# Seeding PSUM banks for Strassen sums in a fused cross-attention and expert FFN kernel

## The chip, the cores and the metric

The kernel runs on one core of a Trainium2 chip. The metric is the device time of one execution in microseconds, taken as the median of several runs.

## The reference

`x` is (16, 112, 256), `ctx` is (16, 375, 256), all in fp32. After a layer norm, one cross attention with biases is added to `x`, and after a second layer norm an expert FFN with 8 experts, all of which see all 1792 tokens:

```python
x = x + xattn(layernorm(x), ctx, Wq, bq, Wk, bk, Wv, bv)
g = einsum('bsh,ehf->ebsf', x_, w_gate)      # x_ = layernorm(x)
u = einsum('bsh,ehf->ebsf', x_, w_up)        # 8 experts, 256 -> 1024
h = silu(g) * u
expert_out = einsum('ebsf,efh->ebsh', h, w_down)
out = einsum('ebsh,bse->bsh', expert_out, cw)  # cw from two softmaxes
```

## The kernel before

**Precision.** Every operand of a matmul is split into a high part (rounded to fp32r) and a low part (the rest), and a product is three matmuls: high x high, high x low, low x high (`three`, `accumulate`, L355). The high part of a tile is a ScalarE copy (`high_...`), the low part a GpSimd subtraction (`low_...`).

**Stages.** An attention stage comes first. The FFN then goes through 64 quads, numbered n. A quad makes the hidden tiles of one pair of 128-wide column blocks of one half expert, for one half of the tokens (two blocks of 448 tokens). Four quads (turn = n mod 4) are one half expert `hn`: turns 0 and 1 are token half 0, turns 2 and 3 token half 1; turns 0 and 2 use one weight set, 1 and 3 the next. Quads 0 to 3 use eight plain products per matrix; quads 4 to 63 use Strassen's seven products P1 to P7, for gate and for up (`product`, L2001). In the text "gate 6" is product P6 of gate.

**Sums.** With Winograd's form of the sums, C11 = P1 + P2, U2 = P1 + P6, U3 = U2 + P7, C22 = U3 + P5, C21 = U3 + P4, C12 = U2 + P5 + P3. Each matrix has three PSUM banks: a, x and y. P1 is made in bank a and P2 is added there by the matmuls, P6, P7 and P4 come in x one behind another, P5 and P3 in y. P1 is copied to SBUF by ScalarE (`gate_first`, `up_first`, through L1060), and VectorE makes five sums per matrix (L1466 to L1503), those of x and y against the tile kept in SBUF. P7, P4 and P3 accumulate on what their bank holds. The hidden tiles are Silu(gate) times up, four per quad (L1505 to L1523, `hidden11` reads C11 of up from PSUM; the other three read two SBUF tiles), then their high part (L1087), then their low part (L702), into one of four `hs` slots.

**Down.** A group g = n // 2 - 1 of two quads is multiplied with the down weights while the next two quads run. For groups 2 to 29 this is four units of 12 matmuls of 448 columns (`unit`, L2072): 0 and 1 in the even quad, 2 and 3 in the odd one. VectorE weighs a unit by the combine weights (L1556) and GpSimd adds it up (L819). The other groups (0, 1, 30, 31) use seven tiles of 12 matmuls of 256 columns (`down`), which VectorE adds up with the weight (L1541). For group 31 each tile is made in two halves, `earlier` (quad 62's part) and `later` (quad 63's part), after the last quad.

**Order.** There is no scheduler: each engine has its own list of calls, written by hand, in a function `quad(n)` (GpSimd L829, ScalarE L1254, VectorE L1763, TensorE L2272), and waits on semaphores stand in the helpers. An instruction that waits holds up all behind it on its engine. TensorE's order in a quad is: gate 1, 6, 5; up 1, 6, 5; unit 2 if n is odd; gate 2, 7; up 2, 7; gate 4, 3; unit 0 if n is even; up 4, 3; unit 3 or 1. ScalarE also makes the high parts of the weight sets (`high_set`, L1017, 1792 columns) and down weights (`high_down`, L1027); GpSimd makes the sums of weights (L681) and the low parts of sets (L691) and of down weights (L696). Weight set 2hn must be ready at turn 0 of half expert hn, set 2hn + 1 at turn 1 (`gate_1_6_5`, L2007). The loads come on SyncE's queue, in program order, each when its buffer is free.

Of the kernel before, what the change touches and what calls it, by code (L numbers as in the profile page):

```python
# [5 lines left out]
def xattn_ffn_kernel(nc, x, ctx, wq, bq, wk, bk, wv, bv, w_router, w_gating, w_gate, w_up, w_down, out):  # L6
# [3 lines left out]
    B, TQ, D = x.shape  # L10
# [38 lines left out]
    LAST = (4, 5, 6, 0, 1, 2, 3)  # L49
# [26 lines left out]
    PROD = {p: i + 1 for i, p in enumerate((1, 6, 5, 2, 7, 4, 3))}  # L76
    U2_SUM, U3_SUM, C22_SUM, C21_SUM, C12_SUM = range(1, 6)
    HID11, HID22, HID21, HID12 = range(1, 5)
# [17 lines left out]
    with es:  # L96
# [90 lines left out]
        u21 = [up_t[:, 0, :], sb("u21_odd", [P, TC])[:, :]]  # L187
        u12 = [up_t[:, 1, :], xsacc[:, TILES * D:TILES * D + TC]]
        g21, g12, g22, g11 = [gate_t[:, i, :] for i in range(4)]
        u22 = up_t[:, 2, :]  # L190

        blocks = [u21[1][:, 0:CB * Q], w_raw0[:, 0, 4:8, :].rearrange("p s f -> p (s f)")[:, 0:CB * Q]]
# [4 lines left out]
        plain_tile = [g11, g12, g21, g22]  # L197
# [70 lines left out]
        ps_end = [ps[:, i, 0:D] for i in (3, 4, 5, 6, 1, 2, 0)]  # L268
# [44 lines left out]
        gate_prod, up_prod, gate_p1, up_p1 = sem("gate_prod"), sem("up_prod"), sem("gate_p1"), sem("up_p1")  # L313
# [17 lines left out]
        def unit_at(g, k):  # L331

            c, block = 1 - k // 2, k % 2
            return acc_t[:, g % CP, block, c * TC:(c + 1) * TC]
# [37 lines left out]
        def _(sp):  # L372
# [222 lines left out]
            for a, b, count in ((4, RT, 3), (0, 2, 5), (2, 3, 6), (3, 4, RT)):  # L595
                sp.wait_ge(acc_done, RT * (CP + 1) + count)
                sp.dma_start(out_v[:, RT + a:RT + b, :], last_acc[1][:, a:b, :]).then_inc(stored, DMA)
            sp.wait_ge(stored, 5 * DMA)
        @block.gpsimd
        def _(pool):  # L600
# [228 lines left out]
            def quad(n):  # L829
# [17 lines left out]
                if turn == 0:  # L847
                    low_set(2 * hn + 1)
                if turn == 1 and hn + 1 < SETS:
# [5 lines left out]
                if turn == 3 and hn + 1 < SETS:  # L855
                    low_set(2 * hn + 2)
# [5 lines left out]
                low_hidden(n, HID22, u22, 1, TC)  # L862
# [3 lines left out]
            low_hidden(QUADS - 1, HID21, u21[1], 0, TC)  # L866
            low_hidden(QUADS - 1, HID12, u12[1], 1, 0)
            add_back(1)
        @block.scalar
        def _(sc):  # L870
# [183 lines left out]
            def before(n, k):  # L1054

                return 4 * n if n == PLAIN else 4 * (n - 1) + k

            def first_product(n, prod, dst, bank, done):
# [3 lines left out]
            def gate_first(n):  # L1062
                if n == PLAIN:
                    sc.wait_ge(hid_lo_done, 4 * n)
                sc.wait_ge(hid_done, before(n, HID21))
                first_product(n, gate_prod, g21, g_a, gate_p1)

            def up_first(n):
                if n > PLAIN + 1:
                    sc.wait_ge(hid_lo_done, 4 * (n - 2) + HID21)  # L1070
                first_product(n, up_prod, u21[n % 2], u_a, up_p1)

            def activate11(n):
                sc.wait_ge(gate_prod, 7 * (n - PLAIN) + PROD[2])
                sc.wait_ge(hid_lo_done, before(n, HID11))
                nc.scalar.activation(g11, g_a, ACT.Silu).then_inc(act_done, 1)  # L1076

            def activate(n, tile, sums):
                sc.wait_ge(gate_sum, 5 * (n - PLAIN) + sums)
# [174 lines left out]
            def quad(n):  # L1254
# [3 lines left out]
                gate_first(n)  # L1258
                if n > PLAIN:
                    high_hidden(n - 1, HID21, u21[(n - 1) % 2], 0, TC)  # L1260
                up_first(n)
                if n > PLAIN:
                    high_hidden(n - 1, HID12, u12[(n - 1) % 2], 1, 0)
                if n == PLAIN:
                    high_part(1, "s13")
                if n == PLAIN + 1:
                    high_part(1, "s2")
                    high_part(1, "s4")
                if turn == 0:
                    high_set(2 * hn + 1)  # L1270
# [1102 lines left out]
```

## Time and profile before

| | |
|---|---|
| median of 3 runs | 964.14 us (962.96 to 965.56) |
| span of the profiled execution | 961.7 us |
| that execution's own time | not given by the page |
| TensorE matmul busy | 956.4 us, 5089 instructions |
| VectorE busy | 744.5 us, 1280 instructions |
| ScalarE busy | 483.2 us, 855 instructions |
| GpSimd busy | 797.4 us, 640 instructions |

The span runs from the first to the last instruction on the chip; the time of a run also holds what lies around it. In a row of a timeline the columns are: start in us from the span's start, length in us, engine and line, operation, output <- inputs, count, and in brackets the idle time of the engine ahead of it with what ended it. PE is TensorE's matmuls, PEld its weight loads, which run beside matmuls, DVE VectorE, ACT ScalarE, POOL GpSimd. An engine's neighbouring instructions can overlap, so that one starts before the one ahead of it has ended.

### The profile page before, as it was taken

The numbers are of one execution on the slowest core, as the hardware profiler recorded it, in microseconds if no ns is written. First come the engines' busy times: TensorE is split into PE (matmuls) and PEld (weight loads), VectorE is DVE, ScalarE is ACT, GpSimd is POOL, SyncE is SP. The second block draws the span as 40 slices with busy tenths as digits, with TensorE's granted clock in tenths as the row PEclk, the third lists the DMA queues.
The fourth block names the chain that finished last, engine by engine and source line by source line (L and its number), as shares of the span: only waits on it lengthen the run. The fifth ranks groups of instructions, "written<-read, shape, count | busy, mean of one in ns | idle before, by whom it ended". The sixth has DMA issues, their size and how long they took to land.

```text
span 961.7 us, 14792 instructions
## 1 busy us (share of the span) xinstructions
PE 956.4 (99%) x5089; PEld 887.8 (92%) x5089; DVE 744.5 (77%) x1280; ACT 483.2 (50%) x855; POOL 797.4 (83%) x640
## 2 busy tenths in 40 slices
PE   9999999999999999999999999999999999999998
PEld 7999899999999999999999999999999999999998
DVE  4997557787877877788877787778877778777995
ACT  6987544454545444444544444445445454445442
POOL 5899976766888888888988888888898888888885
DMA  7472512311010110021100110011100200111135
GB/s 217 119 171 73 145 38 75 109 64 42 22 44 23 42 62 24 22 64 42 44 22 23 45 61 22 23 64 42 45 23 22 74 31 23 36 51 42 39 51 141
DMA packets 73232, 55.85 MB, mean 58 GB/s; under 512 B 30244, under 2 KB 69485, under 8 KB 73158
## 3 DMA queue, kind: packets, MB, share of 16 engines
q1 hardware_dynamic: 73150, 54.91, 19.6%
q8 instruction: 40, 0.66, 0.3%
q14 instruction: 34, 0.28, 0.1%
q10 hardware_dynamic: 8, 0.00, 0.0%
HBM read 46.58 MB, written 6.48 MB: 55 GB/s over the span
## 4 chain that ended last, share of the span: by engine, by line
PE 98%; DMA 1%; ACT 0%; DVE 0%; issue 0%; SPq 0%; DVEq 0%; ACTq 0%
PE ps L355 96%; PE ps L1878 1%; DMA xf<-in_L_xattn_Wk 1%; PE ps L1914 0%; PE ps L1866 0%; PE ps L1931 0%; DVE early L1350 0%; ACT arena L912 0%; PE ps L1957 0%; ACT xf L920 0%; ACT xf L912 0%; ACT early L899 0%; PE ps L1824 0%; DVE arena L366 0%; ACT arena L920 0%
## 5 line engine op out<-in xcount | busy, mean ns | idle before, releaser
L355 PE MATMUL ps<-arena 128*128 128x448 f32 (+5 forms) x2064 | 388.4, 339 | 0.2
L355 PEld LDWEIGHTS ps<-arena 128*128 128x128 f32 (+2 forms) x2064 | 343.6, 186 | 21.4 <-POOL arena L696 0.4
L702 POOL TENSOR_TENSOR arena<-shared,arena 128x448 fp32r<-128x448 f32 x196 | 252.3, 1301 | 120.6 <-ACT arena L1087 116.8
L355 PE MATMUL ps<-xc_hi,w_hi 128*128 128x448 f32 x904 | 330.6, 366 | 0.0
L355 PE MATMUL ps<-xc_hi,w_lo 128*128 128x448 f32 x904 | 330.2, 365 | 0.0
L355 PE MATMUL ps<-xc_lo,w_hi 128*128 128x448 f32 x904 | 330.2, 365 | 0.0
L355 PEld LDWEIGHTS ps<-xc_hi,w_lo 128*128 128x128 f32 x904 | 169.8, 188 | 13.6
L355 PEld LDWEIGHTS ps<-xc_hi,w_hi 128*128 128x128 f32 x904 | 169.8, 188 | 13.3
L355 PEld LDWEIGHTS ps<-xc_lo,w_hi 128*128 128x128 f32 x904 | 169.9, 188 | 13.2
L1080 ACT ACTIVATE shared<-shared 128x448 f32<-128x448 f32 x180 | 101.5, 580 | 145.5 <-DVE shared L1476 73.9
L819 POOL TENSOR_TENSOR xsacc<-xsacc,xf 128x448 f32<-128x448 f32 x104 | 119.3, 1158 | 0.0
L1087 ACT CAST arena<-shared 128x448 fp32r<-128x448 f32 x180 | 101.8, 569 | 27.4 <-DVE shared L1513 27.4
L1060 ACT COPY shared<-ps 128x448 f32<-128x448 f32 x90 | 48.0, 533 | 133.3 <-PE ps L355 106.9
L1556 DVE TENSOR_TENSOR xf<-ps,xf 128x448 f32<-128x448 f32 x104 | 61.9, 617 | 58.7 <-PE ps L355 58.7
L1470 DVE TENSOR_TENSOR shared<-ps,shared 128x448 f32<-128x448 f32 x60 | 37.5, 625 | 48.7 <-PE ps L355 48.7
L1076 ACT ACTIVATE shared<-ps 128x448 f32<-128x448 f32 x60 | 32.8, 546 | 78.9 <-PE ps L355 78.9
L691 POOL TENSOR_TENSOR w_lo<-w_raw,w_hi 128x1792 fp32r<-128x1792 f32 (+1 forms) x17 | 66.1, 3886 | 0.4 <-ACT w_hi L1017 0.4
L1513 DVE TENSOR_TENSOR shared<-shared 128x448 f32<-128x448 f32 x60 | 65.9, 1098 | 0.0
L691 POOL TENSOR_TENSOR w_lo<-early,w_hi 128x1792 fp32r<-128x1792 f32 x15 | 61.2, 4078 | 2.4 <-ACT w_hi L1017 2.4
L1466 DVE TENSOR_TENSOR shared<-ps,shared 128x448 f32<-128x448 f32 x60 | 37.0, 617 | 30.2 <-ACT shared L1060 29.8
L681 POOL TENSOR_TENSOR w_raw<-w_raw 128x256 f32<-128x256 f32 x60 | 46.8, 802 | 1.2
L681 POOL TENSOR_TENSOR early<-early 128x256 f32<-128x256 f32 x60 | 43.7, 750 | 2.4 <-DMA early<-in_L_ffn_w_up 1.2
(168 smaller groups left out, 1154.3 us busy)
## 6 DMA issues: line engine op xcount, KB each, us to landing
early<-in_L_ffn_w_down SPq DMA_DIRECT2D x16, 512.0 KB, 3.8
xf<-cw_dram SPq DMA_DIRECT2D x16, 448.0 KB, 4.7
shared<-in_ctx SPq DMA_DIRECT2D x16, 336.0 KB
w_raw<-in_L_ffn_w_gate SPq DMA_DIRECT2D x17, 256.0 KB, 2.8
w_raw<-in_L_ffn_w_up SPq DMA_DIRECT2D x17, 256.0 KB, 3.2
early<-in_L_ffn_w_gate SPq DMA_DIRECT2D x15, 256.0 KB, 2.9
early<-in_L_ffn_w_up SPq DMA_DIRECT2D x15, 256.0 KB, 3.1
xsacc<-in_x SPq DMA_DIRECT2D x8, 224.0 KB, 6.2
```

Of the source, the lines that this page charges most:

```text
L355: ins = nc.tensor.matmul(dst, w, m, start=first and i == 0, stop=last and i == len(passes) - 1, skip_group_check=onto)
L681: nc.gpsimd.tensor_tensor(s[dst], s[a], s[b], ALU.subtract).then_inc(t_step[n % 2], 1)
L691: nc.gpsimd.tensor_tensor(w_lo[:, n % FPAIRS, :, used, :], raw[:, :, src, :], w_hi[:, n % FPAIRS, :, used, :].bitcast(fp32), ALU.subtract) ...
L702: nc.gpsimd.tensor_tensor(h[:, 1, j, at:at + TC], tile, h[:, 0, j, at:at + TC].bitcast(fp32), ALU.subtract).then_inc(hid_lo_done, 1)
L819: nc.gpsimd.tensor_tensor(to, to, weighed[u % 2], ALU.add).then_inc(unit_done, 1)
L1060: nc.scalar.copy(dst, bank).then_inc(done, 1)
L1080: nc.scalar.activation(tile, tile, ACT.Silu).then_inc(act_done, 1)
L1087: nc.scalar.copy(hs[n % HSLOTS][:, 0, j, at:at + TC], tile).then_inc(hid_hi_done, 1)
L1466: nc.vector.tensor_tensor(g12, g_x, g21, ALU.add).then_inc(gate_sum, 1)
L1470: nc.vector.tensor_tensor(g22, g_x, g21, ALU.add).then_inc(gate_sum, 1)
L1513: nc.vector.tensor_tensor(u22, g22, u22, ALU.mult).then_inc(hid_done, 1)
L1556: nc.vector.tensor_tensor(to, ps_unit[u % 2], cw_all[:, g % CP, c * TC:(c + 1) * TC], ALU.mult).then_inc(weighed_done, 1)
```

## The change

P1 is no longer added by VectorE. ScalarE writes P1 from bank a into bank x (`gate_seed`, `up_seed`), and P6, P7 and P4 all accumulate on it, so x holds U2, then U3, then C21. ScalarE copies P5 out of y (`keep5`) and U2 out of x (`keep2`) into SBUF; P3 accumulates on P5 in y. VectorE makes two sums per matrix: C22 = x + kept P5, C12 = y + kept U2 (up's C12 is written into bank y). Gate's C21 goes to Silu from PSUM, up's C21 and C12 are read by the hidden products from PSUM. Up's x bank gets one extra matmul ahead of its first use (`prime`). The order of the hidden tiles is 11, 22, 12, 21, and units 0 and 1 now make the first token block. Semaphores `gate_kept` and `up_kept` count the three ScalarE copies (SEEDED, KEPT5, KEPT2). The hidden tiles that alternate between two buffers are gate's, not up's.

The core of the diff:

```diff
-    LAST = (4, 5, 6, 0, 1, 2, 3)
+    LAST = (0, 1, 2, 4, 5, 6, 3)
-    PROD = {p: i + 1 for i, p in enumerate((1, 6, 5, 2, 7, 4, 3))}
+    PROD = {p: i + 1 for i, p in enumerate((1, 5, 6, 2, 7, 3, 4))}
...
-            for a, b, count in ((4, RT, 3), (0, 2, 5), (2, 3, 6), (3, 4, RT)):
+            for a, b, count in ((0, 3, 3), (4, 6, 5), (6, RT, 6), (3, 4, RT)):
...
 # GpSimd, quad(n)
                 if n > PLAIN:
-                    low_hidden(n - 1, HID21, u21[(n - 1) % 2], 0, TC)
-                    low_hidden(n - 1, HID12, u12[(n - 1) % 2], 1, 0)
+                    low_hidden(n - 1, HID21, g21, 0, TC)
...
                 low_hidden(n, HID11, g11, 0, 0)
-                low_hidden(n, HID22, u22, 1, TC)
+                low_hidden(n, HID22, g22[n % 2], 1, TC)
+                low_hidden(n, HID12, g12[n % 2], 1, 0)
...
 # ScalarE
+            def seed(n, prod, bank, onto, done):
                 sc.wait_ge(prod, 7 * (n - PLAIN) + PROD[1])
-                nc.scalar.copy(dst, bank).then_inc(done, 1)
+                nc.scalar.copy(onto, bank).then_inc(done, 1)
+            def gate_seed(n):
+                seed(n, gate_prod, g_a, g_x, gate_kept)
+            def up_seed(n):
+                sc.wait_ge(hid_done, 4 * n)
+                seed(n, up_prod, u_a, u_x, up_kept)
+            def gate_keep5(n):
+                sc.wait_ge(gate_prod, 7 * (n - PLAIN) + PROD[5])
+                if n >= PLAIN + 2:
+                    sc.wait_ge(hid_lo_done, 4 * (n - 2) + HID22)
+                nc.scalar.copy(g22[n % 2], g_y).then_inc(gate_kept, 1)
+            def gate_keep2(n):
+                sc.wait_ge(gate_prod, 7 * (n - PLAIN) + PROD[6])
...
+                nc.scalar.copy(g12[n % 2], g_x).then_inc(gate_kept, 1)
...
 # ScalarE, quad(n)
                 if turn == 2 and hn > 1:
                     high_down(hn)
-                gate_first(n)
-                if n > PLAIN:
-                    high_hidden(n - 1, HID21, u21[(n - 1) % 2], 0, TC)
-                up_first(n)
-                if n > PLAIN:
-                    high_hidden(n - 1, HID12, u12[(n - 1) % 2], 1, 0)
+                gate_seed(n)
+                gate_keep5(n)
+                up_seed(n)
+                up_keep5(n)
                 if n == PLAIN:
                     high_part(1, "s13")
+                    high_set(2 * hn + 1)
+                gate_keep2(n)
+                activate11(n)
+                up_keep2(n)
                 if n == PLAIN + 1:
                     high_part(1, "s2")
                     high_part(1, "s4")
-                if turn == 0:
-                    high_set(2 * hn + 1)
-                if turn == 3 and hn + 1 < SETS:
-                    high_set(2 * hn + 2)
+                high_hidden(n, HID11, g11, 0, 0)
                 if turn == 2 and hn == 1:
                     high_down(hn)
-                activate11(n)
-                activate(n, g22, C22_SUM)
-                activate(n, g21, C21_SUM)
-                activate(n, g12, C12_SUM)
-                high_hidden(n, HID11, g11, 0, 0)
-                high_hidden(n, HID22, u22, 1, TC)
+                activate(n, g22[n % 2], C22_SUM)
+                activate(n, g12[n % 2], C12_SUM)
+                high_hidden(n, HID22, g22[n % 2], 1, TC)
+                high_hidden(n, HID12, g12[n % 2], 1, 0)
+                activate21(n)
+                high_hidden(n, HID21, g21, 0, TC)
+                if turn == 2 and hn + 1 < SETS:
+                    high_set(2 * hn + 2)
+                if turn == 3 and hn + 1 < SETS:
+                    high_set(2 * hn + 3)
...
 # VectorE, quad(n)
-                gate_u2(n)
...
                 if odd and g in TURNED:
-                    weigh(g, 0)
                     weigh(g, 1)
+                    weigh(g, 2)
...
-                up_u2(n)
...
-                gate_u3_c22(n)
+                hidden11(n)
+                gate_c22(n)
+                gate_c12(n)
                 if odd and g not in TURNED:
                     add_rows(g, 2, ps_r[2])
                     add_rows(g, 3, ps_r[3])
+                up_c22(n)
+                hidden22(n)
+                up_c12(n)
+                hidden12(n)
                 if n == QUADS - 2:
-                    turn(1, 1)
                     turn(1, 2)
-                up_u3_c22(n)
-                gate_c21_c12(n)
-                hidden11(n)
-                hidden22(n)
...
                     turn(1, 3)
-                up_c21(n)
-                up_c12(n)
+                if not odd and g in TURNED:
+                    weigh(g, 0)
                 hidden21(n)
-                hidden12(n)
...
 # TensorE
-            def gate_2_7(n):
-                pe.wait_ge(gate_p1, n - PLAIN + 1)
+            def gate_6_2(n):
+                pe.wait_ge(gate_kept, 3 * (n - PLAIN) + SEEDED)
+                product(n, 0, 6, g_x, False).then_inc(gate_prod, 1)
                 product(n, 0, 2, g_a, False).then_inc(gate_prod, 1)
+            def gate_7_3(n):
+                pe.wait_ge(gate_kept, 3 * (n - PLAIN) + KEPT2)
                 product(n, 0, 7, g_x, False).then_inc(gate_prod, 1)
+                product(n, 0, 3, g_y, False).then_inc(gate_prod, 1)
+            def gate_4(n):
+                pe.wait_ge(gate_sum, 2 * (n - PLAIN) + C22_SUM)
                 product(n, 0, 4, g_x, False).then_inc(gate_prod, 1)
...
+            def up_4(n):
+                pe.wait_ge(up_sum, 2 * (n - PLAIN) + C22_SUM)
                 product(n, 1, 4, u_x, False).then_inc(up_prod, 1)
...
 # TensorE, quad(n)
-                gate_1_6_5(n)
+                gate_1_5(n)
...
-                up_1_6_5(n)
+                up_1_5(n)
...
                 if odd and turned:
                     unit(g, 2)
-                gate_2_7(n)
+                gate_6_2(n)
                 if odd and by_tile:
                     down(g, 3)
-                up_2_7(n)
-                gate_4_3(n)
+                up_6_2(n)
+                gate_7_3(n)
+                up_7_3(n)
                 if odd and by_tile and n < QUADS - 1:
                     down(g, 4)
                 if not odd and turned:
                     unit(g, 0)
                 if n == QUADS - 2:
                     down(g, 0)
-                up_4_3(n)
+                gate_4(n)
+                up_4(n)
```

After the last quad, TensorE's halves of group 31 come in the order earlier 0, 1, 2, 4; later 0, 1, 2; earlier 5, 6; later 4, 5, 6; earlier 3, later 3, with a wait for the tile that each needs.

## Rows read from the trace of the kernel before

**Rows 1.** The page: busy time, share of the span, instructions.
```profile
PE 956.4 (99%) x5089; PEld 887.8 (92%) x5089; DVE 744.5 (77%) x1280; ACT 483.2 (50%) x855; POOL 797.4 (83%) x640
```

**Rows 2.** Stretches: length, busy us (instructions) of each engine, PEclk, DMA share, GB/s.
```profile
400.00:500.00 100.00, 100.00 (x495) 92.66 (x495) 78.11 (x120) 47.78 (x81) 85.25 (x64) 1.00 0.12 38
...
945.00:961.70 16.70, 14.01 (x117) 13.79 (x115) 8.47 (x16) 2.36 (x5) 10.13 (x11) 1.00 0.39 120
```

**Rows 3.** Waits of TensorE's matmuls, the longest: us in total, times, longest.
```profile
PE ps L1976 <- DVE logits_room L1600: 1.1, 1, 1.1
```

**Rows 4.** Timeline, TensorE: quads 34, 35 and 36 start at 547.15, 560.53, 573.90.
```profile
547.15 0.37 PE L355 MATMUL ps<-xc_hi,w_hi 128*128 128x448 f32 x1
...
567.41 0.19 PEld L355 LDWEIGHTS ps<-xc_hi,w_lo 128*128 128x128 f32 x1
567.62 0.36 PE L355 MATMUL ps<-xc_hi,w_lo 128*128 128x448 f32 x1
...
573.90 0.36 PE L355 MATMUL ps<-xc_hi,w_hi 128*128 128x448 f32 x1
```

**Rows 5.** Timelines of DVE, ACT and POOL over quads 33 to 35.
```profile
541.27 0.63 DVE L1470 TENSOR_TENSOR shared<-ps,shared 128x448 f32<-128x448 f32 x1 [0.59 <-PE ps L355]
541.93 0.62 DVE L1472 TENSOR_TENSOR shared<-ps,shared 128x448 f32<-128x448 f32 x1
...
545.28 0.62 DVE L1513 TENSOR_TENSOR shared<-shared 128x448 f32<-128x448 f32 x1
...
550.44 0.62 DVE L1488 TENSOR_TENSOR shared<-ps,shared 128x448 f32<-128x448 f32 x1 [0.20 <-ACT shared L1060]
...
556.22 1.16 DVE L1513 TENSOR_TENSOR shared<-shared 128x448 f32<-128x448 f32 x1
...
568.02 0.62 DVE L1470 TENSOR_TENSOR shared<-ps,shared 128x448 f32<-128x448 f32 x1 [0.59 <-PE ps L355]
...
542.58 0.58 ACT L1080 ACTIVATE shared<-shared 128x448 f32<-128x448 f32 x1 [1.38 <-DVE shared L1472]
...
549.84 0.53 ACT L1060 COPY shared<-ps 128x448 f32<-128x448 f32 x1 [0.49 <-PE ps L355]
...
563.64 0.57 ACT L1087 CAST arena<-shared 128x448 fp32r<-128x448 f32 x1
564.11 1.70 ACT L1017 CAST w_hi<-early 128x1792 fp32r<-128x1792 f32 x1
...
546.04 2.66 POOL L702 TENSOR_TENSOR arena<-shared,arena 128x448 fp32r<-128x448 f32 x2 [1.09 <-ACT arena L1087]
...
554.75 3.23 POOL L681 TENSOR_TENSOR w_raw<-w_raw 128x256 f32<-128x256 f32 x4
```

**Rows 6.** Three lines by themselves: count, duration in ns (least/median/most), first and last.
```profile
L1513 DVE TENSOR_TENSOR shared<-shared x60: 618/1155/1986, 154.2 to 945.0; 128x448 f32<-128x448 f32 x60
...
L696 POOL TENSOR_TENSOR arena<-early,arena x16: 2407/2791/2802, 121.0 to 923.2; 128x1024 fp32r<-128x1024 f32 x16
...
L702 POOL TENSOR_TENSOR arena<-shared,arena x196: 1142/1159/1639, 99.3 to 946.9; 128x448 fp32r<-128x448 f32 x196
```

**Rows 7.** Timelines of quads 4 (ACT) and 6 (PE, ACT, POOL, PEld).
```profile
146.74 0.94 ACT L994 CAST xc_hi<-xf 128x896 fp32r<-128x896 f32 x1
...
171.27 1.60 PE L355 MATMUL ps<-arena 128*128 128x256 f32 x12
...
176.22 1.05 ACT L1027 CAST arena<-early 128x1024 fp32r<-128x1024 f32 x1 [1.65 <-PE ps L355]
177.35 2.41 POOL L696 TENSOR_TENSOR arena<-early,arena 128x1024 fp32r<-128x1024 f32 x1 [1.54 <-ACT arena L1027]
...
179.81 1.11 PEld L355 LDWEIGHTS ps<-arena 128*128 128x128 f32 x6 [0.41 <-POOL arena L696]
```

**Rows 8.** Timeline of the end: DVE's row additions, and TensorE after the last quad.
```profile
941.00 0.88 DVE L1541 SCALAR_TENSOR_TENSOR early<-ps,cw,early 128x256 f32<-128x256 f32 x2 [0.15 <-PE ps L355]
...
944.45 14.56 PE L355 MATMUL ps<-arena 128*128 128x256 f32 x120
```

More of the change, by code:

```diff
@@ L1063, in gate_first @@
                 if n == PLAIN:
                     sc.wait_ge(hid_lo_done, 4 * n)
[L1065 to L1071, printed above, removed]
+                else:
+                    sc.wait_ge(up_sum, 2 * (n - PLAIN))
+                nc.scalar.copy(u2, u_x).then_inc(up_kept, 1)
@@ L1073, in activate11, with activate21 @@
             def activate11(n):
                 sc.wait_ge(gate_prod, 7 * (n - PLAIN) + PROD[2])
-                sc.wait_ge(hid_lo_done, before(n, HID11))
+                sc.wait_ge(hid_lo_done, 4 * n if n == PLAIN else 4 * (n - 1) + HID11)
                 nc.scalar.activation(g11, g_a, ACT.Silu).then_inc(act_done, 1)
+            def activate21(n):
+                sc.wait_ge(gate_prod, 7 * (n - PLAIN) + PROD[4])
+                sc.wait_ge(hid_lo_done, 4 * n)
+                nc.scalar.activation(g21, g_x, ACT.Silu).then_inc(act_done, 1)
@@ L1785, in quad @@
                     turn(1, 0)
-                if odd and g in TURNED:
-                    weigh(g, 2)
+                    turn(1, 1)
                 if not odd and g - 1 not in TURNED:
                     add_rows(g - 1, 6, ps_r[6])
-                gate_u3_c22(n)
+                hidden11(n)
+                gate_c22(n)
+                gate_c12(n)
                 if odd and g not in TURNED:
@@ L2005, in product, with prime, gate_1_5 @@
                                   first=first, onto=not first)
-            def gate_1_6_5(n):
+            def prime(bank):
+                nc.tensor.matmul(bank, w_hi[:, 0, 0, 0, :], xc_hi[:, 0, 0, :], start=True, stop=True)
+            def gate_1_5(n):
                 hn, turn = n // (CP * FPAIRS), n % (CP * FPAIRS)
@@ L2328, in _ @@
             pe.wait_ge(hid_lo_done, last)
-            pe.wait_ge(gate_sum, 5 * (QUADS - PLAIN))
-            earlier(4)
+            pe.wait_ge(act_done, last + HID11)
+            earlier(0)
+            pe.wait_ge(gate_sum, 2 * (QUADS - PLAIN))
+            earlier(1)
+            pe.wait_ge(hid_done, last + HID11)
+            earlier(2)
+            pe.wait_ge(hid_done, last + HID12)
+            earlier(4)
+            pe.wait_ge(hid_lo_done, last + HID12)
+            later(0)
+            later(1)
+            later(2)
+            pe.wait_ge(act_done, last + HID21)
             earlier(5)
-            pe.wait_ge(act_done, last + HID11)
+            pe.wait_ge(hid_done, last + HID21)
             earlier(6)
-            pe.wait_ge(hid_done, last + HID11)
-            earlier(0)
             pe.wait_ge(hid_lo_done, last + HID21)
@@ L2340, in _ @@
             later(6)
-            pe.wait_ge(up_sum, 5 * (QUADS - PLAIN))
-            earlier(1)
-            earlier(2)
-            pe.wait_ge(hid_lo_done, last + HID12)
-            later(0)
-            later(1)
             pe.wait_ge(acc_done, RT * CP + 6)
             earlier(3)
-            later(2)
             later(3)
```

142 lines of the change are left out of this document (61 added, 81 removed).

## The prediction, made before the changed kernel was run

> **What bounds the kernel now.** I read the page's busy shares first: TensorE is busy 99% of the span [rows 1]. The table of stretches says how full: the granted clock is 1.00, there are about 495 matmuls in each 100 us of the Strassen stage, and idle time only in the last 16.7 us [rows 2]. The list of waits of TensorE has three entries, the longest of 1.1 us, all of them on lines of the attention stage [rows 3]. One wait more, not in that list, shows as a weight load 0.41 us late at 179.81, behind POOL's low part of the down weights [rows 7]. From matmul to matmul it takes 26.75 us / 132 = 0.2027 us over two whole quads [rows 4]. A quad is 14 products of 3 matmuls and two units of 12, so 66 x 0.2027 = 13.38 us, and a product is 0.61. TensorE therefore issues all the time. DVE, ACT and POOL have idle time (77%, 50%, 83% busy), and work taken off them buys nothing unless TensorE waits for it. The change can win almost nothing and can lose wherever an operand of a product comes late. So the question is only: which of the new waits is not met?
>
> **How I put times on the new order.** A few steps, read from rows, carry it. From the start of a product's last matmul to the start of the DVE or ACT instruction that reads it: 567.62 to 568.02, 0.40 [rows 4, 5]. From the start of a DVE sum to one that needs its result: 541.27 to 541.93, 0.66; to an ACT instruction that needs it: 541.93 to 542.58, 0.65 [rows 5]. Independent DVE neighbours follow at 0.53 (two sums of 0.62 overlap) [rows 5]. ACT copy to a dependent DVE sum: 549.84 to 550.44, 0.60 [rows 5]; I take 0.62 behind a Silu. ACT after ACT: the next starts 0.10 before the end, 0.47 behind a high part of 0.57 (563.64 to 564.11), so 0.43 behind a copy of 0.53 [rows 5]. ACT to POOL: 0.08 behind the end (176.22 + 1.05 to 177.35), so 0.65 for a high part [rows 7]. An event on POOL releases the weight load 0.05 later (177.35 + 2.41 = 179.76 to 179.81) [rows 7]; in steady running the weight load starts 0.20 ahead of its matmul [rows 4].
>
> **The part that costs: from an odd quad into the next even one.** The first product that accumulates on a seeded bank, gate 6, must wait for ScalarE's seed. In an even quad nothing stands between up 5 and gate 6, so its first matmul is due 12 x 0.2027 = 2.43 us into the quad, its weight load at 2.23. Counted from the start of the odd quad before it: 78 x 0.2027 - 0.20 = 15.61. In an odd quad unit 2 (12 matmuls) stands ahead of gate 6, so the sums come late, 4.86 us and more after its start. Follow the last of them. Up 7 is products 44 counted in matmuls: its last starts at 8.92, so up's C22 sum starts at 9.32. Hidden 22 follows at 9.98, up's C12 sum at 10.51, hidden 12 at 11.17, high part 12 on ACT at 11.82, Silu 21 behind it at 12.29 (gate 4 was ready at 10.5), hidden 21 on DVE at 12.91, high part 21 at 13.56, and the next ACT instruction at 14.03. In turn 3 (the turn is the quad's number mod 4) that is now the high part of a weight set, which the change moved here from behind up's copy, where it was harmless. It lasts 1.70 [rows 5]: 14.03 + 1.60 = 15.63. Only then comes the gate seed: 0.53, and 0.05 to the weight load: 16.21. Due was 15.61. **TensorE waits 0.60 us.** There are 14 such places (quads 8, 12 ... 60): 14 x 0.60 = 8.4 us. In turn 2 the high part of the down weights stands ahead of the seed instead, 1.05 long [rows 7]: 14.03 + 0.95 + 0.53 + 0.05 = 15.56, met by 0.05. I cost these 14 at nothing; the cover is thin, and each 0.1 us more in the chain makes 1.4 us at them and 1.4 at the others. From an even quad into an odd one unit 2 covers everything: gate 6 is due 2.43 later and the sums come 2.43 earlier.
>
> What is queued behind the late seed on ACT are keep 5, up's seed, keep 5 of up, gate's keep 2. They follow at 0.43 each, and gate 7, due 12 matmuls (2.43 us) after gate 6, still gets its keep in time, since gate 6 itself moved by the same wait.
>
> Two prices in the chain are not shown by a row. The seed writes PSUM, which no ScalarE row of before does: nearest are the copy out of PSUM (0.53) and the same size from SBUF to SBUF (0.57) [rows 5]. I take 0.53, the row with the same source, and bound it by 0.43 and 0.75, since another source moved it by only 0.04; that is -1.4 us (14 places) to +5.5 (28 places, as the turn-2 ones then count too). The Trainium skill (ScalarE: Activation LUTs, Step-by-step) says an ACTIVATE into PSUM is quicker than one into SBUF; by that the seed's price would sit at or below 0.53. It gives no size, and no row here shows it. The second is hidden 22, whose two inputs both lie in SBUF: rows of its kind run from 0.62 to 1.99, median 1.16 [rows 6]. A 0.62 one stands where POOL is between instructions (545.28, POOL idle until 546.04), the 1.16 one beside POOL's weight sums [rows 5]. In the new order POOL's low part 11 starts at 8.79 (up 2's last matmul 7.09, + 0.40, + 0.65, + 0.65) and ends 1.14 to 1.16 later [rows 6] at 9.95 or before, just ahead of 9.98, and low part 22 can't start before hidden 22 is done. So I take 0.62. The Trainium skill (SBUF — State Buffer, two separate sides) calls that shared port an exclusive lock in which the later of the two blocks until the first is done. By that rule an overlap of 0.1 us would cost 0.1, and only a POOL still busy with its weight set would cost 0.5 or more. The rows' 1.16 beside POOL agree with a delay, and a run of four short ones, 3.23 us long, let it in before its end.
>
> **Once only.** (a) Quad 6, down weights of the second half. ACT's high part of them moves from before Silu 11 to behind high part 11. Quad 6 starts at 171.27 - 9 x 0.2027 = 169.45, with two down tiles of 1.45 each in it (12 x 0.12) [rows 7, 8]. Gate 6 now starts 4 products and 2 tiles in, at 5.33; up 2's last matmul at 7.56, hidden 11 at 7.96, high part at 8.61, the down weights' high part at 9.08, POOL's low part at 10.21, its end at 12.62 (2.41; others of its kind take 2.79 [rows 6]), load at 12.67. Due: 5.33 + 24 x 0.2027 - 0.20 = 9.99. Wait 2.7, of which before already has 0.41: **+2.3** (2.7 with the long form). (b) Quad 63: two row additions (0.88 [rows 8]) now stand between gate's C12 sum and up's C22 sum, which up 4 needs at once, with no down tile or unit between. Gate 3's last matmul lies 10 matmuls ahead of up 4, so C12 starts at -1.63, the additions at -1.10, up's C22 at -0.23, its end and load at +0.44, due -0.20: **+0.65**. Quad 5 has the same additions, but a down tile of 1.45 covers them. (c) The priming matmul: **+0.2**. (d) Quad 4: a part and a weight set (0.94 and 1.70 [rows 5, 7]) now stand on ACT ahead of gate's keep 2. Up's keep 5 starts 4.08 in, then 4.51, 5.35, keep 2 at 6.95, end 7.48, load due 7.58: met. (e) The tail: 120 narrow matmuls without a gap [rows 8]. In the new order the last high part 21 is ready about 3.5 us and its low part 4.8 us after up 4, needed after three down tiles and seven half-tiles, over 9 us. The last store is again a single tile behind the last addition, so what follows TensorE's last matmul doesn't change.
>
> **Costed at nothing.** Six sums of 0.62 fewer and four copies of 0.53 more per quad take DVE's busy time down by at least 6 x 60 x 0.62 = 223 us and ACT's up by 4 x 60 x 0.53 = 127 us, to about 610 (63%). POOL's 16 low parts per four quads stay. Its weight sets, sums and units keep their turns, and the high parts that it waits for come earlier, so the loads on SP's queue, which wait for POOL, are not later. The turn of the last rows in quads 61 and 62 falls into DVE's idle time; the copies back have the rest of quad 62 and all of 63.
>
> **Sum.** 8.4 + 2.3 + 0.65 + 0.2 = 11.6 us, on a span of 961.7. The page does not give that execution's own time; the median of the runs is 964.1, 2.4 us above the span, and their spread is 2.6 us. So 964.1 + 11.6 = 975.7.
>
> **The rivals.** (R1, not slower) ScalarE's chain is short enough. Place: the seed ahead of gate 6 in turn 0. It decides at 0.60 us: if the eleven steps from up 7 to the seed are together that much shorter, or TensorE takes the late load up in its queue, no quad waits. With the one-time waits taken up too, the priming matmul alone is left: 964.3; with them 967.3. For it: the steps of before leave TensorE without one wait in 60 quads [rows 2, 3]. Against it: they were read from the same engines at the same sizes, and the wait of 0.41 at 179.81 shows that TensorE does stand when a load is late. (R2, much slower) Hidden 22 runs beside POOL at 1.16. Each odd quad's chain grows by 0.54, then both kinds of boundary wait: 14 x 1.14 + 14 x 0.49 + 3.2 = 26.0, so 990.1. For it: half of the two-SBUF sums of before take that long; against: the POOL gap worked out above, though only 0.03 us wide at its near end. (R3, faster) TensorE paces below 0.2027 because fewer sums and no second PSUM reader disturb it. Before shows the same pace in every stretch of the stage, whatever DVE does, so I give it almost nothing: under 961.
>
> **Chances.** The forecast with its bounds, 970 to 983: 0.60. Between it and R1, or R1's upper end, 966.5 to 970: 0.13. R1 within 0.3%: 0.10. R2 and what lies between, above 983: 0.15. R3: 0.02. A measurement of this kernel tells 0.3% (2.9 us) from no change, so faster 0.02, same 0.10, slower 0.88. The range that leaves 2 in 10 out: 967 to 986.
>
> **What the profile after would show.** Right: the list of TensorE's waits has ACT as releaser, 14 times about 0.6 us, at gate 6 of every fourth quad, and hardly any in turn 2; one of 2.7 at the first unit behind POOL L696's low part; ACT busy about 610, DVE at most 520. The period of four quads grows from 53.5 to 54.1. A wait at turn 2 as well means the chain is longer than I read it; hidden 22 above 0.7 in odd quads means R2. No waits at all and the same pace means R1. Any wait on POOL's hidden low parts, or on gate 7 or up 7, would be a step that I costed at nothing.

## The result, and the profile after

| | before | after |
|---|---|---|
| median of 4 runs | 964.83 us (962.96 to 965.56) | 983.18 us (982.33 to 985.18) |
| span of the profiled execution | 961.7 us | 981.7 us |

The ratio is 1.0202, 95% interval 1.0184 to 1.0219: the changed kernel is 2% slower. The forecast was 975.7, a loss of 11.6 us; the loss is 18.4 by the medians and 20.0 by the spans. (After's profiled execution took 983.44, 1.7 us above its span. If before's also lay 1.7 above its 961.7, it took 963.4, 1.4 under its median; that is the difference between the two losses.) The ratios, here and below, leave out executions that took over 1.5% more than the fastest of the same kernel; where that hides something, single times are given.

The page of the changed kernel: busy time, share of the span, instructions, to be read against [rows 1].

```profile
span 981.7 us, 14972 instructions
PE 968.3 (99%) x5090; PEld 887.6 (90%) x5090; DVE 480.9 (49%) x920; ACT 607.5 (62%) x1095; POOL 764.7 (78%) x640
```

The work went where the forecast put it: DVE falls by 264 us, ACT rises by 124. None of it is time won, because PE, whose busy time even rose, was the bound.

The waits of TensorE's weight loads, after: us in total, times, longest. Before had one in this stage, of 0.41 us [rows 7].

```profile
PEld ps L356 <- ACT ps L1056: 11.4, 18, 0.9
PEld ps L356 <- POOL arena L697: 2.7, 1, 2.7
...
PEld ps L356 <- DVE shared L1504: 0.7, 1, 0.7
```

L1056 is ScalarE's copy of P1 from bank to bank, the seed; L697 POOL's low part of the down weights; L1504 up's C22 sum. The list gives how late a load started. Its matmul is less late than that, since a load starts 0.20 ahead of its matmul in steady running [rows 4] and this lead can be used up.

Stretches, after, with the columns of [rows 2]:

```profile
183.00:190.00 7.00, 6.85 (x26) 6.16 (x27) 2.99 (x5) 2.27 (x5) 6.63 (x8) 0.76 0.65 208
268.00:288.00 20.00, 20.00 (x99) 18.16 (x98) 9.06 (x15) 10.29 (x19) 13.15 (x13) 1.00 0.05 18
400.00:500.00 100.00, 99.29 (x487) 90.78 (x486) 44.78 (x74) 60.48 (x107) 81.58 (x67) 1.00 0.13 42
965.00:981.70 16.70, 13.98 (x117) 13.78 (x115) 5.99 (x12) 1.58 (x3) 8.34 (x10) 1.00 0.35 113
```

Two things stand here that no list of waits shows. In 400 to 500 TensorE did 487 matmuls, not 495; 8 are 1.6 us, but its idle time is 0.71. (Part of the difference is only hidden: a row of 0.37 reaches 0.17 into the next spacing, so each late start shows that much less idle time. The rest is pace.) In 268 to 288 it is never idle and makes 99, where 20 full us of e2_down, further down, hold 101. And 7 us from 183 have a granted clock of 0.76. The tail is as long as before.

**Where the 20.0 us went.** I took the starts of the last 3,940 matmuls of each trace, counted from the end so that they are the same ones (but for six at the near end), and sorted the spacing between neighbours. The priming matmul, quad 5 and the attention stage lie ahead of them and were read by themselves:

| | before | after | forecast of the difference |
|---|---|---|---|
| seed, gate 6 of every fourth quad, 14 places | 0 | 9.3 | 8.4 |
| seed in turn 2, 9 of 0.04 | 0 | 0.4 | 0 |
| unit behind POOL's down weights, quad 6 | 0.30 | 2.60 | 2.3 |
| up 4 of quad 63 | 0 | 0.54 | 0.65 |
| priming matmul | 0 | 0.2 | 0.2 |
| up 5 in quad 5 | 0 | 0.2 | 0 |
| matmuls at half clock | 0 | 1.6 | 0 |
| matmuls at full clock, no wait, spaced 0.2067 and not 0.2027 | 0 | 4.9 | 0 |
| attention stage, ahead of all this | 0 | 0.6 | 0 |
| sum | 0.3 | 20.3 | 11.6 |

The 0.6 is there by the 60th matmul (at 13.14 us before, 13.72 after), in a stage that the change leaves alone, so it is no cost of the change.

**The chain, instruction by instruction.** DVE, ACT and PEld from quad 11 into quad 12, where the forecast had its 0.60 (the columns of a timeline):

```profile
309.47 0.62 DVE L1504 TENSOR_TENSOR shared<-ps,shared 128x448 f32<-128x448 f32 x1
310.20 0.63 DVE L1519 TENSOR_TENSOR g_odd<-g_odd,shared 128x448 f32<-128x448 f32 x1
310.74 0.63 DVE L1509 TENSOR_TENSOR ps<-ps,shared 128x448 f32<-128x448 f32 x1
311.48 0.62 DVE L1524 TENSOR_TENSOR xsacc<-xsacc,ps 128x448 f32<-128x448 f32 x1
...
312.13 0.57 ACT L1116 CAST arena<-xsacc 128x448 fp32r<-128x448 f32 x1 [0.70 <-DVE xsacc L1524]
312.61 0.54 ACT L1105 ACTIVATE shared<-ps 128x448 f32<-128x448 f32 x1
...
313.18 0.62 DVE L1529 TENSOR_TENSOR shared<-shared,ps 128x448 f32<-128x448 f32 x1 [1.08 <-ACT shared L1105]
...
313.83 0.57 ACT L1116 CAST arena<-shared 128x448 fp32r<-128x448 f32 x1 [0.69 <-DVE shared L1529]
314.30 1.69 ACT L1017 CAST w_hi<-w_raw 128x1792 fp32r<-128x1792 f32 x1
315.90 0.52 ACT L1056 COPY ps<-ps 128x448 f32<-128x448 f32 x1
...
316.48 0.19 PEld L356 LDWEIGHTS ps<-xc_hi,w_hi 128*128 128x128 f32 x1 [0.80 <-ACT ps L1056]
```

From up's C22 sum to the seed's end each start follows the one before by 0.73, 0.54, 0.74, 0.65, 0.48, 0.57, 0.65, 0.47, 1.60 and 0.52. The forecast had 0.66, 0.53, 0.66, 0.65, 0.47, 0.62, 0.65, 0.47, 1.60 and 0.53. The two steps from a DVE sum to the DVE sum that needs it are longer, by 0.07 and 0.08, and the one from Silu to DVE is shorter, by 0.05; all together the chain is 0.11 longer. It also started 0.07 later in the quad, at 9.39. So the load came 0.60 + 0.11 + 0.07 = 0.78 late, the row's 0.80. The matmul started at 316.48 where 315.89 was due, 0.59 late, and the one behind it came 0.31 later and not 0.20, so 0.70 is lost: TensorE took up 0.1. Over the 14 places 0.56 to 0.83 is lost, 0.66 on the mean, with loads 0.78 late on the mean. In turn 2 the same 0.18 used up the 0.05 of cover, and the lead hid most of the rest.

Two lines by themselves, after, as in [rows 6]:

```profile
L1519 DVE TENSOR_TENSOR g_odd<-g_odd,shared x30: 625/626/627, 168.9 to 963.8; 128x448 f32<-128x448 f32 x30
...
L1056 ACT COPY ps<-ps x120: 517/517/547, 143.7 to 956.0; 128x448 f32<-128x448 f32 x120
```

Hidden 22 takes 0.63 in all 30 odd quads, in 29 of them with POOL between instructions: R2 did not happen. (In quad 5 it ran beside POOL's weight sums, L682, and still took 0.625.) In the even quads, where nothing hangs on it, the same line takes 0.63 to 2.40, the longest beside POOL's low part of the down weights, which ended at 183.10:

```profile
181.19 2.40 DVE L1519 TENSOR_TENSOR shared<-shared 128x448 f32<-128x448 f32 x1 [0.23 <-ACT shared L1109]
```

The seed costs 0.52, against 0.53 assumed; the sentence of the Trainium skill (ScalarE: Activation LUTs, Step-by-step) that a write to PSUM is the quicker one agrees, with 0.015 us.

ACT, POOL and PEld in quad 6, after:

```profile
179.16 0.57 ACT L1116 CAST arena<-shared 128x448 fp32r<-128x448 f32 x1 [0.80 <-DVE shared L1514]
179.64 1.04 ACT L1027 CAST arena<-early 128x1024 fp32r<-128x1024 f32 x1
...
180.76 2.34 POOL L697 TENSOR_TENSOR arena<-early,arena 128x1024 fp32r<-128x1024 f32 x1 [4.66 <-ACT arena L1027]
...
183.15 3.51 PEld L356 LDWEIGHTS ps<-arena 128*128 128x128 f32 x12 [2.70 <-POOL arena L697]
```

The wait is the 2.7 of the forecast. What was not in it is the length of the row: 12 loads in 3.51 us, 0.29 each and not 0.20. The granted clock is 0.50 from 184.0 to 187.4, the lower of the two levels, 1.2 GHz. It fell 0.9 us after TensorE had started again behind 2.70 us of idleness.

### The profile page after: what moved, and what is told of

It is laid out like the page before. It is cut to its first block, busy times and chain, and to the rows that moved or that the text cites. A ratio compares the mean times of both kernels' runs of the same rounds, so it can differ in the third digit from the quotient of the medians.

```text
span 981.7 us, 14972 instructions
## 1 busy us (share of the span) xinstructions
PE 968.3 (99%) x5090; PEld 887.6 (90%) x5090; DVE 480.9 (49%) x920; ACT 607.5 (62%) x1095; POOL 764.7 (78%) x640
## 4 chain that ended last, share of the span: by engine, by line
PE 89%; DVE 5%; ACT 3%; issue 3%; DMA 1%; POOL 0%; SPq 0%; DVEq 0%; ACTq 0%
PE ps L356 86%; ACT w_hi L1017 1%; PE ps L1880 1%; ACT ps L1056 1%; DVE shared L1504 1%; DVE shared L1514 1%; DVE ps L1509 1%; DVE xsacc L1524 1%; DVE shared L1529 1%; DVE g_odd L1494 1%; DMA xf<-in_L_xattn_Wk 1%; DVE xsacc L1499 1%; ACT shared L1105 1%; PE ps L1916 0%; PE ps L1868 0%
## 5 line engine op out<-in xcount | busy, mean ns | idle before, releaser
L703 POOL TENSOR_TENSOR arena<-shared,arena 128x448 fp32r<-128x448 f32 x196 | 225.8, 1164 | 98.8 <-ACT arena L1116 93.5
L356 PEld LDWEIGHTS ps<-xc_hi,w_lo 128*128 128x128 f32 x904 | 169.7, 188 | 14.8
L1562 DVE TENSOR_TENSOR xf<-ps,xf 128x448 f32<-128x448 f32 x104 | 64.9, 624 | 163.1 <-PE ps L356 163.1
L1514 DVE TENSOR_TENSOR shared<-shared,ps 128x448 f32<-128x448 f32 x60 | 37.3, 621 | 195.9 <-PE ps L356 193.9
L1056 ACT COPY ps<-ps 128x448 f32<-128x448 f32 x120 | 62.8, 524 | 35.6 <-PE ps L356 31.0
L703 POOL TENSOR_TENSOR arena<-g_odd,arena 128x448 fp32r<-128x448 f32 x30 | 34.8, 1158 | 41.6 <-ACT arena L1116 41.6
L1529 DVE TENSOR_TENSOR shared<-shared,ps 128x448 f32<-128x448 f32 x60 | 37.3, 622 | 52.6 <-ACT shared L1105 35.0
L1087 ACT COPY xsacc<-ps 128x448 f32<-128x448 f32 x30 | 16.0, 534 | 70.8 <-PE ps L356 70.6
L697 POOL TENSOR_TENSOR arena<-early,arena 128x1024 fp32r<-128x1024 f32 x16 | 38.4, 2398 | 25.5 <-ACT arena L1027 25.5
L682 POOL TENSOR_TENSOR w_raw<-w_raw 128x256 f32<-128x256 f32 x60 | 48.1, 824 | 1.2
L682 POOL TENSOR_TENSOR early<-early 128x256 f32<-128x256 f32 x60 | 43.4, 745 | 1.2
```

The costliest lines, as they stand in the source:

```text
L356: ins = nc.tensor.matmul(dst, w, m, start=first and i == 0, stop=last and i == len(passes) - 1, skip_group_check=onto)
L682: nc.gpsimd.tensor_tensor(s[dst], s[a], s[b], ALU.subtract).then_inc(t_step[n % 2], 1)
L697: nc.gpsimd.tensor_tensor(wd[:, 1, :, :], wd_raw, wd[:, 0, :, :].bitcast(fp32), ALU.subtract).then_inc(wd_done, 1)
L703: nc.gpsimd.tensor_tensor(h[:, 1, j, at:at + TC], tile, h[:, 0, j, at:at + TC].bitcast(fp32), ALU.subtract).then_inc(hid_lo_done, 1)
L1056: nc.scalar.copy(onto, bank).then_inc(done, 1)
L1087: nc.scalar.copy(g12[n % 2], g_x).then_inc(gate_kept, 1)
```

## The experiments

Theory of the waits: each place of the table is one cause by itself and can be taken away by itself; without them the new kernel has the time of before. (Times of the experiments are to be compared through their ratios: the executions of before that ran beside them have medians of 963.3 and 963.4, not 964.8.) For the 4.9 us of pace there were two: **writes** (a second engine writes PSUM beside the matmuls and slows them), and **re-timing** (a late weight load alone sets another spacing).

**e1_set.** The weight set's high part leaves turn 3 for turn 0, behind up's keep 2:

```diff
                 up_keep2(n)
+                if turn == 0 and hn > 1:
+                    high_set(2 * hn + 1)
...
-                if turn == 3 and hn + 1 < SETS:
-                    high_set(2 * hn + 3)
```

> After, with the high part of every second weight set taken from the end of turn 3 and put into turn 0, behind up's keep 2. If ScalarE's queue ahead of the seed is the cause, the waits at gate 6 of quads 8, 12 ... 60 (0.57 to 0.83 each, 9.3 us in all) go, and the time falls to 974 or below; if the seed was late for another reason, they stay and the time is 983. On the pace of the matmuls (0.2027 us between two before; after the change 0.2067 in about a third of the Strassen stage, 4.9 us in all) there are two theories. Re-timing: the slow spacing follows a late weight load, so most of it goes too, and the time is 969 to 971. PSUM writes: it comes from ScalarE writing the banks, so it stays, and the time is about 974.

975.65 us (974.28 to 977.15), ratio 1.0131 (1.0116 to 1.0146); span 973.3. PEld's waits:

```profile
PEld ps L356 <- POOL arena L697: 2.7, 1, 2.7
...
PEld ps L356 <- ACT ps L1056: 0.5, 3, 0.2
```

The 14 waits are gone, 9.3 us of them, but the time falls by only 7.5. The waits and the half clock account for 5.0 of this span, the spacing of 0.2067 for 6.7, more than after had. So fewer waits do not mean less of the slow pace. Neither theory's time came: re-timing had 969 to 971, writes 974, and the pace that stayed speaks for writes, if for either. It takes the kernels of before, below, to tell them apart.

**e2_down.** The down weights' high part in quad 6 earlier:

```diff
+                if turn == 2 and hn == 1:
+                    high_down(hn)
                 gate_keep2(n)
...
                 high_hidden(n, HID11, g11, 0, 0)
-                if turn == 2 and hn == 1:
-                    high_down(hn)
```

> After, with the high part of the down weights of quad 6 put ahead of gate's keep 2 instead of behind high part 11. If that place made the one wait of 2.5 us at the first unit, it goes, and with it the stretch of 3.4 us at half clock that follows it (9 matmuls 0.17 late each, 1.6 us): 983.2 - 2.3 - 1.6 = 979.3. If the half-clock stretch has another cause it stays, and the time is 980.9.

977.27 us (976.11 to 978.67), ratio 1.0146 (1.0132 to 1.0159); span 976.2. The stretch of quads 6 and 7:

```profile
180.00:200.00 20.00, 20.00 (x101) 18.53 (x100) 10.04 (x17) 11.23 (x20) 13.91 (x11) 1.00 0.30 97
```

Clock 1.00 and no idle time. The same stretch of after:

```profile
180.00:200.00 20.00, 17.68 (x79) 15.67 (x78) 8.35 (x12) 9.79 (x17) 14.11 (x11) 0.91 0.30 99
```

One edit took away the wait and the half clock together, 4.2 us by the traces (2.6 and 1.6): the half clock belongs to that wait. Single executions agree: the mean granted clock is 0.998 in all four of after and of e1_set, 1.000 in all four of e2_down. The median is 2 us below the 979.3 forecast, and 1.5 of that is that before too ran faster beside it (963.3 for 964.8). The other 1.3 us of the span are 0.8 of earlier starts, pace (0.2) and small waits, none of which the edit touched.

**e3_all.** Both edits, and two more:

```diff
+                gate_seed(n)
                 if turn == 2 and hn > 1:
                     high_down(hn)
-                gate_seed(n)
...
+                up_c22(n)
                 if odd and g not in TURNED:
                     add_rows(g, 2, ps_r[2])
                     add_rows(g, 3, ps_r[3])
-                up_c22(n)
```

> After, with both of these moves, the seed ahead of the down weights' high part in turn 2, and up's C22 sum ahead of the row additions in quads 5 and 63. No wait of TensorE is left but 0.2 at quad 5 and the priming matmul. Re-timing theory of the pace: 0.2027 throughout, 983.2 - 9.3 - 0.3 - 3.9 - 0.5 - 4.9 = 964.3, the time of before. PSUM-write theory: the slow pace stays, 969. In both, the whole loss was order and pace, and taking work off VectorE gained nothing.

963.80 us (963.04 to 972.02, 12 executions), ratio 1.0037 (1.0011 to 1.0063). The median says that the theory of the waits is right. But single executions fall into two heaps: 7 at 963.0 to 963.9, 5 at 971.0 to 972.0. The profiled one is of the second, span 969.2. Stretches of it:

```profile
400.00:500.00 100.00, 100.00 (x495) 92.68 (x495) 50.45 (x74) 62.10 (x113) 81.10 (x63) 1.00 0.12 38
600.00:700.00 100.00, 100.00 (x486) 90.83 (x485) 50.14 (x73) 62.83 (x111) 80.69 (x63) 1.00 0.12 41
```

Both full, both at clock 1.00, but 9 matmuls fewer in the second. Where does it turn? DVE and PE at 515 us:

```profile
514.95 0.62 DVE L1494 TENSOR_TENSOR g_odd<-ps,g_odd 128x448 f32<-128x448 f32 x1 [0.34 <-issue]
...
516.02 0.61 DVE L1504 TENSOR_TENSOR shared<-ps,shared 128x448 f32<-128x448 f32 x1
...
516.35 0.36 PE L356 MATMUL ps<-xc_lo,w_hi 128*128 128x448 f32 x1
516.55 0.37 PE L356 MATMUL ps<-xc_hi,w_lo 128*128 128x448 f32 x1
516.76 0.40 PE L356 MATMUL ps<-xc_hi,w_hi 128*128 128x448 f32 x1
517.00 0.37 PE L356 MATMUL ps<-xc_lo,w_hi 128*128 128x448 f32 x1
```

DVE once started 0.34 late with nothing that it waited for. Up's C22 sum came out at 516.63, and the first load of up 4 started at 516.68 where 516.56 was due. One spacing of 0.24 is all that TensorE shows. From there to the end of the stage every spacing is 0.2067: 8.1 us, which is the distance between the heaps.

The hole is no accident of this execution. It stands at the same instruction, L1494 in quad 35, in the traces of all five kernels with the change, and in none of the four without it. In e1_set:

```profile
522.23 0.62 DVE L1494 TENSOR_TENSOR g_odd<-ps,g_odd 128x448 f32<-128x448 f32 x1 [0.35 <-issue]
...
523.67 0.19 PEld L356 LDWEIGHTS ps<-xc_hi,w_lo 128*128 128x128 f32 x1
523.97 0.19 PEld L356 LDWEIGHTS ps<-xc_hi,w_hi 128*128 128x128 f32 x1
```

There up 4's load came 0.30 behind the one before it, 0.09 late. No matmul was late by it, but the spacing turned at it all the same, here from 0.2067 back to 0.2027, and so it did in after and e2_down. What makes the hole is open.

**b1_wait.** The kernel of before, with TensorE made to wait for the high part of the turn-0 weight set at up 2 (`w_hi_done` counts the parts). It has no seed and no ScalarE write to PSUM:

```diff
             def up_2_7(n):
+                if n % (CP * FPAIRS) == 0 and n >= 2 * CP * FPAIRS:
+                    pe.wait_ge(w_hi_done, FPAIRS * (n // (CP * FPAIRS)) + 2)
```

> The kernel before, with nothing of the change, but TensorE waits ahead of up 2 in quads 8, 12 ... 60 for the high part of the weight set that ScalarE makes in that quad: by the rows of before that is 0.6 us late each time, 14 x 0.6 = 8.4 us, so 973.2. Re-timing theory of the pace: stretches at 0.2067 appear here too, behind these waits, and add 2 to 5 us: 975 to 978. PSUM-write theory: ScalarE writes no bank here, the pace stays 0.2027 and the time 973.

973.72 us (972.42 to 974.13), ratio 1.0106 (1.0093 to 1.0119); span 971.9. Its waits of PEld, and a stretch:

```profile
PEld ps L355 <- ACT w_hi L1017: 9.4, 14, 0.7
...
270.00:300.00 30.00, 30.00 (x147) 27.24 (x146) 22.17 (x35) 13.79 (x24) 24.57 (x24) 1.00 0.06 18
```

14 late loads of 0.64 to 0.69 put into before cost 10.4 us by the medians, 10.2 by the spans: 7.9 of waits and 2.5 of pace. The stretch shows it, with 147 matmuls: 30 us hold 148 at 0.2027 and 145 at 0.2067, and each count takes in about two more at its edges. The slow stretches (179.2 to 204.3, 258.3 to 313.4, 637.8 to 693.0) start and end at a late load; the first starts at the load of quad 6, 0.41 late, which before has as well. So the writes into PSUM are not needed for the slow pace; late loads are enough. The time alone would have misled: 973.7 is what the writes theory had (973), since the waits cost 0.5 less than forecast; it is the trace that decides.

**b2_down and b3_down.** Before again, with one single load made late: the down weights' high part of quad 6 behind Silu 11, or behind Silu 22 too.

```diff
-                if turn == 2 and hn == 1:
-                    high_down(hn)
                 activate11(n)
+                if turn == 2 and hn == 1:
+                    high_down(hn)
                 activate(n, g22, C22_SUM)
```

(in b3_down the call stands one line lower.)

> The kernel before, with the high part of the down weights of quad 6 behind Silu 11 instead of ahead of it. By the rows of before this makes the load of the first unit 1.6 us late instead of 0.41, once: +1.2, 964.5. If the half-clock stretch needs an idle time as long as the 2.5 to 2.7 of the changed kernel, the clock stays 1.00. On the pace: if a late load can leave the matmuls at 0.2067 and nothing later sets them back, single runs come out near 965 or up to 16 us above it, and few between; if the slow pace belongs to the change, all are 964 to 966.

> The kernel before, with the same high part behind the Silu of C22: the first unit's load 3.4 us late by the rows of before, once, so +3.0. If a long idle time of TensorE is what lets the granted clock fall, a stretch at half clock follows here too, some 1.6 us more: 968. If the fall belongs to the change (ScalarE's PSUM writes, more work at once), the clock stays 1.00 and the time is 966. The pace as in b2_down.

b2_down: the load is 1.37 late, against 0.41. Single executions are 7 at 963.85 to 966.14 and 6 at 978.6 to 981.2; the ratio 1.0008 (0.9998 to 1.0018) covers the lower heap alone. The profiled one took 979.31, of the upper heap. Its wait, and a stretch 620 us later:

```profile
PEld ps L355 <- POOL arena L696: 1.4, 1, 1.4
...
800.00:900.00 100.00, 100.00 (x486) 90.83 (x485) 78.09 (x120) 45.91 (x80) 81.55 (x65) 1.00 0.13 41
```

After that one wait, at 180.85, the spacing is 0.2067 for all the rest of the stage: 14.8 us. With the 1.0 of longer wait this is the whole distance of its span (977.5) from before's. The clock stays at 1.00.

b3_down: 981.05 us (967.08 to 984.67, 6 executions), ratio 1.0108 (1.0054 to 1.0163), which mixes two executions near 967 with two near 981. The load is 3.30 late. Its wait, and the 7 us behind it:

```profile
PEld ps L355 <- POOL arena L696: 3.3, 1, 3.3
...
183.00:190.00 7.00, 5.10 (x18) 4.62 (x19) 2.70 (x4) 1.83 (x4) 6.92 (x7) 0.76 0.56 159
```

Again 3.4 us at a granted clock of 0.50, in the kernel of before: the half clock follows an idle time of 2.7 or 3.3, and did not follow 1.37 or less in any of these traces. Behind it the slow pace holds to the end, 14.7 us. Two executions of six (967.1 and 967.5) were without it, so the same wait does not always bring it. Nor does it always bring the half clock: the mean granted clock is 0.998 in four of the six, those two among them, and 1.000 in the other two (980.9 and 981.2).

**e5_order.** e3_all left up 4's sum with no room. Here TensorE makes gate's P3 behind up 7, and VectorE makes up's C22 ahead of gate's C12:

```diff
                 gate_c22(n)
-                gate_c12(n)
                 up_c22(n)
+                gate_c12(n)
...
                 product(n, 0, 7, g_x, False).then_inc(gate_prod, 1)
+
+            def gate_3(n):
                 product(n, 0, 3, g_y, False).then_inc(gate_prod, 1)
...
                 product(n, 1, 7, u_x, False).then_inc(up_prod, 1)
+                gate_3(n)
                 product(n, 1, 3, u_y, False).then_inc(up_prod, 1)
```

> e3_all, with TensorE's gate 3 behind up 7, and on VectorE up's C22 sum ahead of gate's C12. Its profile showed no late load but one of 0.04 us at up 4 in quad 35, behind a hole of 0.34 in VectorE's issue, and the slow pace from there to the end. With this order up's C22 sum starts 0.6 us earlier and up 4 is covered by about 1.0 instead of 0.37, so such a hole is absorbed. If late loads are what starts the slow pace, no wide gap and no slow stretch is left and the time is 963.5; if the pace changes by itself, slow stretches come as before.

963.01 us (962.70 to 965.79, 11 executions, one heap), ratio 0.9999 (0.9991 to 1.0008); span 961.1. The page and a stretch:

```profile
PE 956.4 (100%) x5090; PEld 888.0 (92%) x5090; DVE 515.4 (54%) x920; ACT 606.8 (63%) x1095; POOL 769.1 (80%) x640
...
800.00:900.00 100.00, 100.00 (x495) 92.70 (x494) 47.20 (x74) 63.86 (x114) 82.07 (x68) 1.00 0.14 43
```

No late load in the Strassen quads but one of 0.3 in quad 4, and no slow stretch. VectorE's hole of 0.34 is there (L1494, at 515.01), and the load of up 4 is on time behind it, as forecast. All of the change's new sums and seeds are in it, with all of ScalarE's writes to PSUM, and TensorE's busy time is that of before to the last digit. So the whole loss came from order, none from the seeding itself; and 229 us less on DVE buy nothing. (One heap in 11 executions does not show that the slow pace can't come here: before has it in 5 of 42, see below.)

## Why the prediction was right and where it was short

**The size**: the direction is right and the time lies inside the range of 967 to 986, but 0.2 above the band of 970 to 983 that had 0.60; it fell where only 0.15 was given. The terms that were argued came out at 12.3 us for 11.6. What brings the loss to 20.0 are terms that the argument did not have.

**The bound**: right. TensorE sets the time in every version, and with all waits gone the changed kernel runs exactly like before (e5_order).

**The seed in turn 0** (8.4 us): right in mechanism, places and releaser, and shown by e1_set. The term came out at 9.3. Two errors half cancel: the step "from the start of a DVE sum to one that needs its result, 0.66" was mis-sized for these pairs, 0.73 and 0.74, which with the later start makes the load 0.8 late; and a late load was taken to cost as much as it is late, where TensorE takes up 0.1 on the mean. (The 0.53 between independent DVE neighbours is cited from rows that don't show such a pair; the chain above has it, 0.54.)

**Turn 2** ("costed at nothing; the cover is thin"): nearly right in size, 0.4 us in all, but the 0.05 of cover was not there. **Quad 6**: 2.3 as forecast. **Quad 63**: 0.54 for 0.65. **Quad 5**: 0.2, which the argument left out:

```profile
PEld ps L356 <- DVE cw_rows L1572: 0.3, 1, 0.3
```

L1572 is VectorE's copy of the combine weights out of up's y bank, once in the kernel. Up 5 needs that bank and is now up's second product, not its third, so the copy is due 0.61 earlier; the argument looked only at the down tile's cover for the additions. The steps costed at nothing on gate 7, up 7, the hidden low parts and the tail cost nothing; no such wait is in the list.

**What failed** is the step under R3: "before shows the same pace in every stretch of the stage, whatever DVE does", and with it the silent rule that a late load costs what it is late and no more. Before had one late load of 0.41 in the stage and none in the other quads, so its trace could not show what one does to those behind it. Late loads cost 4.9 us of slower spacing in after, on top, and 1.6 us of half clock behind the longest. These two are 6.5 of the 8.4 us that the forecast is short by the spans; 0.9 is the seed's term; the rest are quad 5, turn 2 and the 0.6 of the attention stage.

**The rivals**: R1 (no wait) fell: the chain was longer, not shorter, and TensorE took up only 0.1 of a late load. R2 fell by L1519's row. The Trainium skill's exclusive lock (SBUF — State Buffer, two separate sides) was no more than a threat on the chain, as POOL had its gap there in 29 of the 30 odd quads; the even quads' 2.40 at 181.19, which ended 0.48 behind POOL's low part, agrees with it, and quad 5's 0.625 beside POOL shows no block. R3 had the right subject, the pace, and the wrong sign.

Still open: what decides, at a late load, which of the two spacings TensorE takes. The same load 1.37 late led to either in b2_down. A late load stands at the change even where no gap between matmuls shows it: the three slow stretches of e1_set end (523.9, 664.2, 881.4) at up 4 of quad 35, shown above, and at two loads of gate 6 in turn 2 that start 0.215 and 0.214 behind the one before, where the pace is 0.207.

## What to carry to other kernels

When one engine is full, moving work off the others is worth nothing and the order of what it waits for is worth everything: count the chain to each operand against when it is due, and give it some tenths of a microsecond of room, not 0.05, since the chain's steps are known to 0.07 and an engine can start 0.34 late where no row says why. A wait of a matmul stream can cost more than its length. If single executions of a kernel fall into two heaps about 1 or 2% apart, compare the matmul counts of equal, fully busy stretches before looking at anything else.

## What the runs showed of the hardware that was not expected

**Two spacings at the full clock.** Matmuls of 128x128 by 128x448 follow each other at 202.67 ns (starts by 203, 199, 207, 202 in turn) or at 206.67 ns (207, 207, 206), whatever the operands, at a granted clock of 1.00. A stream keeps its spacing for tens to hundreds of microseconds, and every lasting change of it inside the Strassen stage stands within six matmuls of a load that came late, or right behind the half clock. About half of the late loads change nothing. Loads that turned it were late by as little as 0.01 us (the two at gate 6 in e1_set), and one 1.37 us late held it slow for 765 us (b2_down). Before has executions of this kind as well by their times: beside b2_down 2 of 25 took 977.5 and 978.1, the others 962.8 to 965.9, and beside e1_set 3 of 17 took 977.7, 978.1 and 980.3, the others 962.8 to 963.9. No trace of one was taken, but b1_wait's trace shows the one late load that before has, 0.41 in quad 6, turn the spacing.

**The half clock.** With a single idle time of 2.70 us (after, e1_set) or 3.30 us (b3_down) came 3.4 us at a granted clock of 0.50, worth 1.4 to 1.6 us. In after it began 0.9 us behind the end of the idle time, in b3_down 0.4 ahead of it. With an idle time of 1.37 (b2_down) it did not come. By the mean clocks of single executions it came in 12 of the 14 with an idle time of 2.7 or 3.3, in none of the 44 of the other changed or delayed kernels, and in 1 of 42 of before.

**Small ones.** A ScalarE copy of 128x448 from PSUM takes 0.517 us to PSUM and 0.53 to SBUF. The mean of POOL's 196 low parts (shared tile) fell from 1.301 us before (L702) to 1.164 after (L703), with both medians at 1.159, where DVE makes far fewer sums out of SBUF alone; whether that is the cause was not tried.
